# First attention of a fused four-stage block: the band mask of the row maxima added on VectorE, five of fifteen NF4 comparisons as Sign on ScalarE, x normalised on ScalarE

## The reference, cut to what matters

```python
x = x + L0_xattn(layernorm(x), ctx_2048, ...)      # the stage that changes
x = x + L0_ffn(layernorm(x), weight1..3)           # weights first go through nf4_roundtrip
x = x + L1_xattn(layernorm(x), ctx_2048, ...)
x = x + L1_ffn(layernorm(x), ...)                  # mixture of experts

def L0_xattn(mask, encodings, w_in, b_in, w_out, b_out, w_ct, b_ct, local_size=64):
    q, k, v = split(transpose(mask) @ w_in.T + b_in)         # 8 heads of 16
    scores = einsum('bqhd,bkhd->bhqk', q, k) / sqrt(16)
    band = abs(idx[:, None] - idx[None, :]) <= local_size
    scores = where(band, scores, finfo.min)
    attn = softmax(scores)
    o = einsum('bhqk,bkhd->bqhd', attn, v) @ w_out.T + b_out
    y = relu(transpose(o)) * encodings
    return einsum('nit,io->not', y, w_ct) + b_ct

def nf4_quantize(w):                                         # blocks of 64 values
    scaled = blocks / scalers_1[:, None]                     # by each block's largest magnitude
    idx = argmin(abs(scaled[:, None] - NF4))                 # one of 16 levels
```

## Time and profile before

| | us |
|---|---|
| median of 3 runs | 1593.83 (1593.65 to 1594.47) |
| profiled execution | 1597.84 |
| its span in the profile | 1596.1 |

### The profile page before, as it was taken

The page is one execution under the profiler, slowest core; times in us unless marked ns, Lnnn a source line. Parts: engine busy times, 40 slices in busy tenths (PEclk is TensorE's granted clock), DMA queues, the critical chain, the costliest instruction groups (busy, mean ns, idle before and its releaser), DMA issues. The chain is left out here.

```text
span 1596.1 us, 27584 instructions
## 1 busy us (share of the span) xinstructions
PE 1415.8 (89%) x8734; PEld 850.6 (53%) x8832; DVE 1045.1 (65%) x2732; ACT 642.0 (40%) x1452; POOL 223.2 (14%) x252
## 2 busy tenths in 40 slices
PE   2489999999999889999978999998589899999995
PEld 1245555555555444444445565555334577777773
DVE  6788898898998655455554787877577644444310
ACT  4344444444444453332236666666320122222221
POOL 2100000000000000000020000010010255555553
PEclk8699999999999999999998999999799999999998
DMA  8423323323322120000000000000411378888884
GB/s 277 74 74 105 90 74 106 87 75 104 87 84 57 47 80 1 0 0 0 1 27 28 14 15 14 13 1 1 173 53 53 129 221 239 238 235 242 234 249 93
DMA packets 76246, 147.44 MB, mean 92 GB/s; under 512 B 13700, under 2 KB 43236, under 8 KB 71952
## 3 DMA queue, kind: packets, MB, share of 16 engines
q1 hardware_dynamic: 63552, 116.78, 23.0%
q0 software_dynamic: 12624, 29.77, 8.4%
HBM read 112.16 MB, written 34.34 MB: 92 GB/s over the span
## 5 line engine op out<-in xcount | busy, mean ns | idle before, releaser
L309 ACT ACTIVATE probs_t<-ps_sc 128x512 f32<-128x512 f32 x256 | 152.9, 597 | 275.5 <-PE ps_sc L407 273.4
L632 DVE TENSOR_REDUCE row_max<-ps_max 128x2 f32<-128x384 f32 (+1 forms) x256 | 158.4, 620 | 48.6 <-PE ps_max L390 48.2
L1025 PE MATMUL f_ps<-f_xt,w_t 128*128 (+1 forms) x704 | 158.5, 379 | 4.7 <-DVE f_xt L970 2.4
L2413 DVE TENSOR_TENSOR d_inter<-d_silu_g,d_su 128x384 f32<-128x384 f32 x32 | 17.7, 554 | 190.0 <-PE d_su L2158 183.3
L737 DVE TENSOR_SCALAR nf_above<-nf_scaled 128x512 f16<-128x512 bf16 x495 | 119.9, 282 | 0.0
L451 PE MATMUL ps_nf<-nf_above,ident_f 128*128 128x512 f16 x363 | 115.9, 384 | 0.0
L1025 PEld LDWEIGHTS f_ps<-f_xt,w_t 128*128 128x128 bf16 x704 | 68.8, 98 | 87.3 <-issue 4.3
L2170 PE MATMUL d_sy<-d_wdown,d_inter 128*96 128x512 f32 x256 | 115.0, 592 | 0.0
L1608 ACT ACTIVATE c_probs<-c_s,c_negmax 128x128 f32<-128x128 f32 x256 | 90.4, 365 | 56.5 <-DVE c_negmax L1693 55.8
L387 PE MATMUL ps_max<-band_mask,identb 128*128 128x384 bf16 (+1 forms) x198 | 71.4, 360 | 36.4 <-DMA k_stack<-dr_parts 18.0
L2031 POOL DMA_INDIRECT out<-d_h,d_scatter_now x64 | 93.2, 1456 | 55.2 <-ACT d_h L2250 29.6
(11 more groups left out here) (309 smaller groups left out, 2577.2 us busy)
## 6 DMA issues: line engine op xcount, KB each, us to landing
d_wgu<-in_ex_gu SPq DMA_DIRECT2D x32, 1024.0 KB, 7.1
d_wdown<-in_ex_d SPq DMA_DIRECT2D x32, 512.0 KB, 3.7
dr_parts<-qk_parts SPq DMA_DIRECT2D x16, 768.0 KB, 3.4
q_stack<-dr_parts SPq DMA_DIRECT2D x192, 64.0 KB, 2.8
k_stack<-dr_parts SPq DMA_DIRECT2D x192, 64.0 KB, 2.9
out<-x_sb SPq DMA_DIRECT2D x17, 256.0 KB, 3.0
nf_w<-in_nf_w POOLq DMA_DIRECT2D x3, 1408.0 KB, 14.7
x_sb<-in_x SPq DMA_DIRECT2D x4, 1024.0 KB, 6.7
```

The source lines that it names most:

```text
L309: act.activation(pt[:, c, :], SP[c % 2][:].rearrange("p a w -> p (a w)"), ACT.Exp, scale=D0 ** -0.5).then_inc(s_e, 1)
L632: dve.tensor_reduce(mx[:, g, 8 * hp + qt:8 * hp + qt + QT + 1:QT], M[c % 2][:, :, off:off + hi - lo], AX.X, ALU.max).then_inc(s_mx, 1)
L1025: mm = pe.matmul(bank[:], w12[:, m, kt, ft * P:(ft + 1) * P], xt[:, q, kt, bass.ds(g * N, N)], start=(kt == 0 and q == 0), stop=(kt == KT ...
```

## The change

- `smax` drops its mask matmul. VectorE keeps the band mask itself: `take_max` becomes two `tensor_tensor_reduce`, one for each head of the bank (192 or 256 columns), which add the mask, write the sum as bf16 into a new buffer and give the maximum through an accumulator output. Before them stand a wait for VectorE's own result of two steps before and a `nop`.
- Of the 15 comparisons, numbers 10 to 14 become Sign activations on ScalarE with a bias from a table (`nf4_sign`), spread after certain `exps` (`SIGN_AT`). TensorE multiplies their arrays with an identity scaled by half the step's height, and waits for them where it adds number 10. The base level changes to `SIGN_BASE`. VectorE makes two comparisons in each of steps 0 to 4, and the adding of eight arrays to four moves to step 5.
- `norm_x(i + 2)` goes from VectorE to ScalarE, as Identity with scale and bias from tables; VectorE computes the table of biases (`nmr`) in the prologue. The first two images are still normalised on VectorE.
- `v_copy` is one instruction instead of four. `nf4_scale` becomes a `scalar_tensor_tensor`. Before the reciprocal of the block maxima stands one with a lower bound. Five scaled identities and five biases are made in the prologue. After the last image five Signs stand before the last `relu`.

```diff
+NDV = 10
+TINY = 1.2e-38
+def between(step):
+    return step + 2.0 ** (math.frexp(step)[1] - 9)
+SIGN_BASE = LEVELS[0] + sum((LEVELS[k + 1] - LEVELS[k]) / 2 for k in range(NDV, NLV))
...
+    SIGN_AT = [[[10], [11], [], [], [], [], [12], [13, 14]], [[10], [], [11], [], [], [12], [13], [14]]]
...
+            def norm_x(i, b):                                   # scalar
+                ge(act, s_proj, 2 * i - 2)
+                ge(act, s_vp, i - 1)
+                act.activation(xn[:, b, :], x[:, i, :], ACT.Identity, bias=nmr[:, i, :], scale=rstd[:, i, :]).then_inc(s_xn, 1)
+            def nf4_sign(m, g, k):
+                if k == NDV:
+                    act.wait_ge(s_lv, m + 1)
+                    ge(act, s_lm, m - 1)
+                act.activation(above[:, g, k, :], lvl[:, g, :], ACT.Sign, bias=cut[:, k - NDV:k - NDV + 1]).then_inc(s_sg, 1)
...
             def body(j, i, b, first, last, final):              # scalar
+                if not last:
+                    norm_x(i + 2, b)
                 for c in range(8):
                     exps(2 * i, c)
+                    for k in SIGN_AT[0][c]:
+                        nf4_sign(2 * i, 0, k)
...
             o_copy(2 * NB - 1, 1)
             ot_copy(NB - 1)
+            for k in range(NDV, NLV):
+                nf4_sign(NCH - 1, 0, k)
             relu(NB - 1)
...
-                pe.matmul(m[:, :, off:off + hi - lo], identb[:], mask[:, :, off:off + hi - lo], start=True, stop=False)
                 for k in range(2):
                     h = 4 * g + 2 * hp + k
                     mm = pe.matmul(m[:, k, off:off + hi - lo], qst[0:96, b, h, BAND + qt * P:BAND + qt * P + P],
-                                   kst[0:96, b, h, lo:hi], start=False, stop=(k == 1))
+                                   kst[0:96, b, h, lo:hi], start=True, stop=True)
...
+                if NDV in ks:
+                    pe.wait_ge(s_sg, NSG * m + NSG)
                 for k in ks:
-                    mm = pe.matmul(NF[:], ident16[:], above[:, g, k, :], ...)
+                    mm = pe.matmul(NF[:], ident16[:] if k < NDV else half16[:, k - NDV, :], above[:, g, k, :], ...)
...
-                for t in range(QT):                             # v_copy
-                    op = dve.tensor_tensor(va[:, b, t, :, 0:D0], ...)
+                dve.tensor_tensor(va[:, b, :, :, 0:D0], G[0][:]..., bv_row[:]..., ALU.add).then_inc(s_v, 1)
...
-                dve.tensor_reduce(mx[:, g, 8 * hp + qt:8 * hp + qt + QT + 1:QT], M[c % 2][:, :, off:off + hi - lo],
-                                  AX.X, ALU.max).then_inc(s_mx, 1)
+                ge(dve, s_mx, 8 * u + c - 1)
+                dve.nop(nofuse=True)
+                for k in range(2):
+                    at = 8 * hp + QT * k + qt
+                    op = dve.tensor_tensor_reduce(masked[:, c % 2, k, off:off + hi - lo], M[c % 2][:, k, off:off + hi - lo], mask[:, k, off:off + hi - lo],
+                                                  1.0, -3e38, ALU.add, ALU.max, mx[:, g, at:at + 1])
+                op.then_inc(s_mx, 1)
...
+            for k in range(NDV, NLV):                           # vector, after the cast of the identity
+                dve.tensor_scalar(half16[:, k - NDV, :], ident[:], (LEVELS[k + 1] - LEVELS[k]) / 2, None, ALU.mult).then_inc(s_i16, 1)
+                dve.memset(cut[:, k - NDV:k - NDV + 1], -between(STEPS[k])).then_inc(s_cut, 1)
...
-            chain(dve.reciprocal(rsc1[:], sc1[:]))
+            chain(dve.tensor_scalar(rsc1[:], sc1[:], TINY, None, ALU.max))
+            chain(dve.reciprocal(rsc1[:], rsc1[:]))
...
+                ge(dve, s_sg, NSG * (m - 1))                    # nf4_scale
-                dve.tensor_tensor(blocked(lvl[:, g, :]), columns(m), of_block(rsc1, m), ALU.mult)
+                dve.scalar_tensor_tensor(out=blocked(lvl[:, g, :]), in0=columns(m), scalar=-TINY, in1=of_block(rsc1, m),
+                                         op0=ALU.add, op1=ALU.mult)
...
-                for k in range(2 * c, min(2 * c + 2, NLV)):
+                if c < 5:
+                    for k in range(2 * c, 2 * c + 2):
...
             def body(j, i, b, first, last, final):              # vector
-                if not last:
-                    norm_x(i + 2, b)
```

More of the change, by code:

```diff
@@ L10 @@
+import math
 from contextlib import ExitStack
@@ L116, in phase_layer0_attention @@
     ident16 = sb("ident_f16", [P, P], F16)
+    half16 = sb("nf4_half_step", [P, NLV - NDV, P], F16)
+    cut = sb("nf4_sign_at", [P, NLV - NDV], F32)
+    nmr = sb("neg_mean_rstd", [P, NB, 1], F32)
+    masked = sb("masked_scores", [P, 2, 2, WIN], BF16)
     ones = T["ones"]
@@ L141, in phase_layer0_attention @@
     s_abs, s_fold = sem("a_nf4_magnitudes"), sem("a_nf4_fold")
+    s_sg, s_cut, s_nmr = sem("a_nf4_sign"), sem("a_nf4_sign_at"), sem("a_neg_mean_rstd")
     s_i16, s_lv, s_ab, s_lm, s_nw = sem("a_ident_f16"), sem("a_nf4_scaled"), sem("a_nf4_above"), sem("a_nf4_mm"), sem("a_nf4_done")
@@ L171, in phase_layer0_attention @@
     blocks = [(0, 8), (1, 8), (2, 22)]
-    NF_INC = 9
+    NF_INC = 6
+    NSG = NLV - NDV
     nb = CH // BLK
@@ L339, in _ @@
                            ACT.Copy).then_inc(s_ko, 1)
+            act.wait_ge(s_cut, NSG)
+            act.wait_ge(s_nmr, 2)
             def body(j, i, b, first, last, final):
+                if not last:
+                    norm_x(i + 2, b)
                 for c in range(8):
                     exps(2 * i, c)
+                    for k in SIGN_AT[0][c]:
+                        nf4_sign(2 * i, 0, k)
                     if c == 2 and not first:
@@ L351, in body @@
                     exps(2 * i + 1, c)
+                    for k in SIGN_AT[1][c]:
+                        nf4_sign(2 * i + 1, 1, k)
                     if c == 1 and not first:
@@ L449, in nf4_sum @@
                     ge(pe, s_nw, m)
+                if NDV in ks:
+                    pe.wait_ge(s_sg, NSG * m + NSG)
                 for k in ks:
-                    mm = pe.matmul(NF[:], ident16[:], above[:, g, k, :], start=(k == 0), stop=(k == NLV - 1), skip_group_check=True)
+                    mm = pe.matmul(NF[:], ident16[:] if k < NDV else half16[:, k - NDV, :], above[:, g, k, :], start=(k == 0), stop=(k == NLV - 1), skip_group_check=True)
                 if ks[-1] == NLV - 1:
@@ L561, in body @@
                         ct(i - 1)
-            pe.wait_ge(s_i16, 1)
+            pe.wait_ge(s_i16, 1 + NSG)
             pe.wait_ge(s_ko, 1)
@@ L592, in row_stats @@
                 dve.wait_ge(s_rstd, k + 1)
+                dve.scalar_tensor_tensor(out=nmr[:, lo:hi], in0=mv[:, lo:hi, 0:1], scalar=-1.0, in1=rstd[:, lo:hi],
+                                         op0=ALU.mult, op1=ALU.mult).then_inc(s_nmr, 1)
             row_stats(0, 0, FIRST)
@@ L620, in v_copy @@
                 ge(dve, s_pv, 4 * i - 4)
-                for t in range(QT):
-                    op = dve.tensor_tensor(va[:, b, t, :, 0:D0], G[0][:, t * P:(t + 1) * P].rearrange("p (h d) -> p h d", d=D0),
-                                           bv_row[:].rearrange("p (h d) -> p h d", d=D0), ALU.add)
-                op.then_inc(s_v, 1)
+                dve.tensor_tensor(va[:, b, :, :, 0:D0], G[0][:].rearrange("p (t h d) -> p t h d", t=QT, d=D0),
+                                  bv_row[:].rearrange("p (o h d) -> p o h d", o=1, d=D0).broadcast_to((P, QT, H0, D0)),
+                                  ALU.add).then_inc(s_v, 1)
             def take_max(u, g, c):
@@ L728, in nf4_scale @@
                 ge(dve, s_ab, NF_INC * (m - 1))
-                dve.tensor_tensor(blocked(lvl[:, g, :]), columns(m), of_block(rsc1, m), ALU.mult).then_inc(s_lv, 1)
+                ge(dve, s_sg, NSG * (m - 1))
+                dve.scalar_tensor_tensor(out=blocked(lvl[:, g, :]), in0=columns(m), scalar=-TINY, in1=of_block(rsc1, m),
+                                         op0=ALU.add, op1=ALU.mult).then_inc(s_lv, 1)
             def nf4_compare(m, g, c):
@@ L735, in nf4_compare @@
                     ge(dve, s_lm, m - 1)
-                for k in range(2 * c, min(2 * c + 2, NLV)):
-                    op = dve.tensor_scalar(above[:, g, k, :], lvl[:, g, :], STEPS[k], LEVELS[k + 1] - LEVELS[k], ALU.is_gt, ALU.mult)
-                op.then_inc(s_ab, 1)
-                if c == 4:
+                if c < 5:
+                    for k in range(2 * c, 2 * c + 2):
+                        op = dve.tensor_scalar(above[:, g, k, :], lvl[:, g, :], STEPS[k], LEVELS[k + 1] - LEVELS[k], ALU.is_gt, ALU.mult)
+                    op.then_inc(s_ab, 1)
+                if c == 5:
                     dve.wait_ge(s_ab, NF_INC * m + 4)
@@ L746, in nf4_weight @@
                 dve.wait_ge(s_repr, 48)
-                dve.scalar_tensor_tensor(out=columns(m), in0=blocked(NF[:]), scalar=LEVELS[0], in1=of_block(rep, m),
+                dve.scalar_tensor_tensor(out=columns(m), in0=blocked(NF[:]), scalar=SIGN_BASE, in1=of_block(rep, m),
```

## The result

The changed kernel takes 1604.69 us (median of 4 runs, 1603.97 to 1608.67), the kernel before beside it 1594.15 (4 runs): ratio 1.0071, 95% interval 1.0053 to 1.0088, so 0.7% slower. Its profiled execution took 1604.02 us, with a span of 1602.3. The first attention ends at 560.9 us instead of 552.0 (start of the last `nf_wmax` reduction on VectorE), and the other three stages keep their 1041 to 1044 us, so the loss is made in the first one.

The account below looks back on a forecast made before the run. Bound: in each image VectorE's part A, then a chain of transfers, part B. 14 images x -0.6 = -8.4, with -2.0 + 0.8 + 1.6 gives -8.0 us: 1597.84 profiled becomes 1589.8, median 4.0 lower, 1586 us; range 1574 to 1614.

Parts of the forecast that it names:

- rival 2: r is 0 to 0.03, TensorE bounds part A at about 14.6 us; image 28.45 us, 1575 us; chance 0.16.
- Rival 1: r is 0.11 or more, VectorE becomes the bound; 0.15 gives 1615 us, 0.25 gives 1663 us; chance 0.23.
- the five rivals: Slower 0.23, faster 0.16, no difference 0.13, Sign table loads 0.02, ScalarE's queue delaying scores or parts 0.06.
- r: Price on VectorE of getting the maximum out of each take_max instruction, 32 times an image; taken as 0.08 us.
- Part A: From an image's first matmul to its last third_part, nearly filled by VectorE; forecast 15.25 us instead of 15.96.
- The pairs: Two instructions replacing each take_max reduction: 0.54 us a pair at 192 columns, 0.68 at 256, without r.
- Part B: From the write to dr_parts to the next image's first matmul, a chain of transfers; stays 13.85 us.
- TensorE's idle time ahead of the image's start: At the image's border, before the start behind q_stack<-dr_max: over a microsecond forecast, some tenths before the change.
- nop and wait: Before each take_max; the nop delays starts by 0.07 us at three places of part A, 0.2 us.
- ScalarE: Ten Signs and one Identity an image at 0.69 us each, 7.6 us; 21 of 29 us in all.
- Prologue: norm_x of image 2 no longer waits for block scales, -2.0 us; ten constants delay the first write, +0.8 us.
- Tail: The last chunk's five Signs stand between ot_copy and the last relu: +1.6 us, hidden by nothing.

Follow-up runs that it names:

- a_shift28: The changed kernel with 28 one-column memsets on VectorE ahead of its first work, loop unchanged: 1575.31 us, ratio to the kernel before 0.9862.
- b_chain: The kernel before with the write to dr_max issued after eight of the twelve stack transfers instead of after all: 1592.12 us, ratio 0.9977.
- b_long: The kernel before with three more already-met waits in front of every take_max reduction, VectorE's loop 309 instructions instead of 247: 1596.50 us, ratio 1.0005.
- a_shift64: The changed kernel with 64 one-column memsets on VectorE ahead of its first work, loop unchanged: 1587.60 us, ratio to the kernel before 0.9953.
- b_long_moved: The kernel before with three more met waits before every take_max reduction and 60 one-column memsets ahead on VectorE: 1610.37 us, ratio 1.0091.
- b_mask: The kernel before with only smax and take_max changed (band mask added on VectorE) and VectorE's loop written out: 1605.12 us, ratio 1.0054.

## Why the prediction was wrong

1586 us was forecast, faster; 1604.7 came, slower. By its steps:
- What failed is the sum: it priced each instruction by its engine's time and had no term for the length of VectorE's loop. The length could be counted from the kernel's text, 247 instructions and 100 more, on an engine nearly full; its price no row of the kernel before could show, since that kernel has no such stall. The cost is 26.3 us over five jumps (the five long images of the changed kernel less the same five of a_shift28), of the 26.4 us between the ends of their first stages. It is the main part of the step from 0.986 to 1.007; between the medians lie 29.4 us, and the last 3 us no profile shows. Without it the forecast would have erred by 14 us the other way: 0.9862 of 1594.15 is 1572 us, close to rival 2's 1575.
- Rival 1 was "slower" by another mechanism (a dear accumulator read), and none of the five rivals was this one. That 1604.7 lies in the range has nothing to do with the reason given for its upper end.
- r was taken as 0.08 and is 0: the read's duration was right (0.08 us), but it takes no slot. What ScalarE's row shows, a slot of its own for the read, isn't so on VectorE.
- Part A was forecast at 15.25 us; in a_shift28 it is 14.41 (246.32 to 260.73), by rival 2 14.6. The pairs are 0.55 and 0.68, as worked out.
- Part B stays at 13.8 us (232.50 to 246.32), as forecast, but its reading was wrong in one sentence: "no engine's work shortens B", and that the chain sets the time. TensorE does start behind read-backs, but b_chain takes 1.8 us out of the chain and the image keeps its 29.70 us. The two limits lay within tenths of each other, and regular gaps behind an issue looked like proof of one.
- TensorE's idle time ahead of the image's start: forecast over a microsecond, measured 1.04 in the mean in a_shift28 (12.5 us in 12 waits for dr_max's read).
- nop and wait: 0.2 us an image forecast. In b_long 96 met waits a round cost nothing; the nop by itself no run shows.
- ScalarE: a Sign 0.69 us forecast, 0.72 measured (136 of them from 104 to 520 us); the Identity of `norm_x`, 0.69 forecast, took 0.81. No further table load and no wait of TensorE for its queue: right.
- Prologue: -1.2 us forecast; the third write to dr_parts, the first for which an image's own steps count, is at 85.07 instead of 88.32: -3.3. Tail: +1.6 forecast, 3.55 less 1.81 is +1.7: right.

## What to carry to other kernels

Count the instructions of a loop's body on each engine, waits and register instructions included, before pricing what they do: by the count of blocks that these runs bear out, a body of up to some 257 instructions on VectorE stays in place wherever it begins and one of 347 only if it begins in the first 37 instructions of a block of 128. Measured were a body of 347 at three places and one of 309 at two; where it lay on four blocks, each round cost 2.2 to 7 us. Idle time put down to "issue" behind a jump, together with instruction packets at a steady period, is the sign; here a few instructions ahead of the loop, or writing it out on that engine, was the remedy. And a limit read from a steady gap behind one wait should be tested by shortening that wait's chain, since the next limit can lie a tenth of a microsecond behind.

## What the runs showed of the hardware

- Instruction code came in packets of 8192 bytes, five in each round of a loop that lies on four blocks. A stall at the jump was 2.7 to 3.1 us, a second one 1.9 to 2.4 us where the block ended some ten instructions behind the jump's target. With 33 or 74 instructions left in the block there was one only.
- The price in the image was 2.2 us (a_shift64), 2.3 to 4.3 (b_long_moved) and 3.9 to 7.0 (changed). The dearest come with a granted clock of 0.90 and 0.95 in their stretch, as the fourth window row above shows against the second. In the fourth TensorE waits 3.86 us for nf_w, up to 318.28 us, and its granted clock is 0.50 (1.2 GHz) from 317 to 323 us. The second has such a wait too (3.40 us) and stays at 1.00.
- VectorE's accumulator read is an instruction of 0.08 us that lies wholly beside the next one.
- Where the place of code decides, an edit anywhere ahead of the loop on the same engine changes the time: 28 memsets of one column were worth 2.1% (0.9862 against 1.0071).
- A lower clock can hide what a change is worth: in b_mask images of the same busy time on VectorE (28.2 us) took 29.26 us at a granted clock of 1.00 and 30.85 us at 0.94.
